# One core, four blocks: decay rows by broadcast DMA, tail decay on the keys, half-size fillers, another step order

## The reference

```python
mixed = jax.nn.silu(_causal_conv(hidden @ w_qkv, conv_w))      # q, k: 16 heads of 128; v: 32 heads of 128
g = -jnp.exp(A_log) * jax.nn.softplus(a + dt_bias)             # one decay per token and value head
def step(state, xs):
    q_t, k_t, v_t, g_t, b_t = xs
    state = state * jnp.exp(g_t)[..., None, None]
    kv = jnp.einsum('bhk,bhkv->bhv', k_t, state)
    delta = (v_t - kv) * b_t[..., None]
    state = state + jnp.einsum('bhk,bhv->bhkv', k_t, delta)
    out = jnp.einsum('bhk,bhkv->bhv', q_t, state)
    return (state, out)
# out * silu(z), RMS norm, times norm_gamma, @ w_out
```

## Time and profile before

| | before |
|---|---|
| median of three executions | 1450.89 us |
| profiled execution | 1452.2 us, its span 1450.4 us |
| TensorE (PE) busy | 1304.9 us, 90% |
| weight loads (PEld) busy, beside PE | 872.4 us, 60% |
| VectorE (DVE) busy | 962.6 us, 66% |
| ScalarE (ACT) busy | 792.2 us, 55% |
| GpSimd (POOL) busy | 750.8 us, 52% |
| mean granted TensorE clock | 0.973 of full speed |
| step 0 up to the first scan product | to 96.6 us |
| steps 1 to 16 | 96.6 to 1036 us |
| the other three blocks | the remaining 414 us |

### The profile page before, as it was taken

How to read it: one execution, slowest core, us unless ns; L and a number is a source line. 1 busy time by engine, 2 the same in 40 slices (tenths; PEclk the granted TensorE clock), 3 DMA queues, 4 the chain that set the end, 5 groups by cost and what they waited for, 6 DMA issues and landing times. The chain is left out here.

```text
span 1450.4 us, 24932 instructions
## 1 busy us (share of the span) xinstructions
PE 1304.9 (90%) x8680; PEld 872.4 (60%) x8680; DVE 962.6 (66%) x1918; ACT 792.2 (55%) x1944; POOL 750.8 (52%) x1245
## 2 busy tenths in 40 slices
PE   6768999999999999999999999988898899899893
PEld 4356666666666666666666666665545466545672
DVE  5847778787787877878778787774602366641454
ACT  3546676666766667666666666665432365420120
POOL 1675776857758667585676856761000000117363
PEclk9969999999999999999999999999999999999997
DMA  2534355354453544535445354364201950202687
GB/s 81 134 64 114 64 152 142 90 150 113 133 138 93 150 117 128 143 88 150 117 129 143 88 150 117 114 145 157 66 0 27 374 160 1 81 13 104 137 185 185
DMA packets 233180, 171.71 MB, mean 118 GB/s; under 512 B 163746, under 2 KB 202998, under 8 KB 230240
## 3 DMA queue, kind: packets, MB, share of 16 engines
q1 hardware_dynamic: 226912, 161.59, 41.3%
q0 software_dynamic: 6144, 8.53, 3.3%
HBM read 104.64 MB, written 65.83 MB: 118 GB/s over the span
## 5 line engine op out<-in xcount | busy, mean ns | idle before, releaser
L1267 DVE SCALAR_TENSOR_TENSOR heads_y<-psum_banks,gdn_conv_w,heads_y 128x1021 f32<-128x1021 f32 (+2 forms) x192 | 244.6, 1275 | 11.3 <-ACT heads_y L1072 6.8
L776 PE MATMUL psum_banks<-main_hT,gdn_w_in 128*128 128x512 f32 x512 | 242.6, 608 | 6.1 <-DMA gdn_w_in<-in_w_in 4.0
L1562 POOL TENSOR_TENSOR heads_XT<-heads_XT,heads_tmp 128x126 f32<-128x126 f32 (+22 forms) x496 | 205.6, 414 | 38.9
L1559 POOL TENSOR_TENSOR heads_tmp<-heads_XT,heads_A 128x126 f32<-128x126 f32 (+22 forms) x496 | 180.7, 364 | 39.8
L776 PEld LDWEIGHTS psum_banks<-main_hT,gdn_w_in 128*128 128x128 f32 x512 | 97.0, 195 | 95.8 <-issue 91.5
L1530 POOL TENSOR_TENSOR heads_og<-heads_og,heads_fac 128x512 f32<-128x512 f32 x60 | 60.5, 1039 | 138.7 <-DVE heads_fac L1333 138.7
L890 PE MATMUL psum_banks<-heads_w_z,main_hT 128*128 128x256 f32 x512 | 122.9, 383 | 0.0
L1095 ACT ACTIVATE heads_O<-psum_banks,heads_coef 128x128 f32<-128x128 f32 x224 | 69.9, 364 | 95.8 <-PE psum_banks L807 95.4
L1072 ACT ACTIVATE heads_y<-psum_banks,gdn_conv_w 128x1024 f32<-128x1024 f32 x64 | 71.4, 1116 | 89.6 <-PE psum_banks L776 89.6
L1288 DVE SCALAR_TENSOR_TENSOR heads_S<-heads_S,heads_coef,psum_banks 128x128 f32<-128x128 f32 x192 | 57.4, 340 | 85.6 <-PE psum_banks L830 85.2
L1278 DVE SCALAR_TENSOR_TENSOR heads_X<-psum_banks,heads_coef,heads_v_s 128x128 f32<-128x128 f32 x224 | 67.9, 345 | 65.3 <-PE psum_banks L805 65.3
(11 more groups left out here) (291 smaller groups left out, 2994.9 us busy)
## 6 DMA issues: line engine op xcount, KB each, us to landing
values_by_tokens<-heads_v_s SPq DMA_DIRECT2D x64, 256.0 KB, 4.1
heads_v_s<-values_by_tokens SPq DMA_DIRECT2D x16, 1024.0 KB, 5.6
outputs_by_features<-heads_ogT SPq DMA_DIRECT2D x120, 128.0 KB, 2.4
heads_ogT<-outputs_by_features SPq DMA_DIRECT2D x30, 512.0 KB, 3.7
main_w_gu<-in_w_gu SPq DMA_DIRECT2D x4, 2816.0 KB, 21.1
gdn_w_in<-in_w_in SPq DMA_DIRECT2D x16, 512.0 KB, 5.3
heads_A<-kk_blocks SPq DMA_DIRECT2D x64, 128.0 KB, 4.8
keys_by_tokens<-heads_k_tok SPq DMA_DIRECT2D x64, 128.0 KB, 3.3
```

The source lines that it names most:

```text
L776: ins = pe.matmul(out[:, half * 512:(half + 1) * 512], w_in[:, kd_, j * P:(j + 1) * P], hT[:, kd_, half * 512:(half + 1) * 512], start=kd_ ...
L1267: dve.scalar_tensor_tensor(y[j][:, shift:T], src[:, 0:T - shift], conv_w[:, head, j, t:t + 1], y[j][:, shift:T], ALU.mult, ALU.add).then_i ...
L1559: pool.tensor_tensor(tmp[:, 0:n, 0:m], bc_last(XT[:, 0:n, j], m), bc_mid(A0[:, j, j + 1:BLK], n), ALU.mult).then_inc(solve_step.sem, 1)
L1562: pool.tensor_tensor(XT[:, 0:n, j + 1:BLK], XT[:, 0:n, j + 1:BLK], tmp[:, 0:n, 0:m], ALU.add).then_inc(solve_step.sem, 1)
```

## The change

Four things are changed, all in the steps:

1. The cumulated sums of head h come by one transfer that copies the row of 2048 numbers to all 128 partitions, straight into `Dm`. The 16 matmuls of `decay0` to `decay3` are gone. VectorE adds the mask in place, from and to SBUF. ScalarE applies exp with a bias for each partition (the negative sum), so in 16 instructions of 128 columns, not 4 of 512. The transfer waits until the inverse of the head before is done with `Dm`, and is first in a step's transfer order.
2. The tail decay is put on the keys: ScalarE makes `k_tail` from the keys of the chunk ahead of its need, Dt is gone, and the state update is two products of 128 columns with two sets of weights, where it was one of 256.
3. Projections, gate products and output products may be split in two (`p0.0`, `p0.1`), to stand in two rows.
4. The order tables of TensorE, ScalarE, VectorE, GpSimd and the transfers are other ones.

```diff
 PE_PLAN = banked(rows("""
-0: z0/0
-1: p0/-1 p1/-1
-3: z1/1
-4: z2/2 norm_q/3
-5: p2/-1
-6: decay0/3 decay1/2 decay2/0 decay3/1
+0: z0/3 p0.0/-1
+1: p0.1/-1 p1.0/-1
+2: p1.1/-1
...
 ACT_PLAN = rows("""
-7: kk0 exp0 kk1 exp1
-10: exp2 exp3 gamma
+9: kk1 exp0
+10: exp1 y6a
+14: diagonal exp2 u6a norms
+15: exp3
...
 DVE_PLAN = rows("""
-5: vt1 decay0 decay1 decay2
-6: decay3
-8: tap10 tap11 tap12 factors turn
+6: decay0 vt1 decay1
+7: factors norm_q tap10
+8: tap11
+9: turn tap12
+10: decay2 decay3
...
-20: inverse0 out0 tap31 out1
-22: out2 tap32 inverse1 out3
+20: attn1 tap31
+21: inverse0 inverse1
+22: tap32 out0 out1 out2 out3
...
+SP_PLAN = """gates inverse_out inverse_in values_out products_out values_in products_in outputs_out0 kt_out outputs_in0 outputs_out1 w_z kt_in outputs_in1 w_in w_o""".split()
+POOL_PLAN = """pow norm0 norm1 q_root norm2 scale norm3 solve""".split()
...
             def gate_rows(h):
-                for sign, rows in enumerate([row_to, row_from]):
-                    src = cum_rows[sign, IT * h:IT * (h + 1)].rearrange("(g s) t -> g s t", g=4)
-                    sp.dma_start(rows[h % 2][sign:P:32], src).then_inc(s_rows[h % 2], 16)
+                src = cum_rows[IT * h:IT * (h + 1)].rearrange("(o s) t -> o (s t)", o=1)
+                sp.dma_start(flat(Dm[:]), src.to_broadcast([P, IT * P])).then_inc(rows_in.sem, 16)
...
                     if c < C - 1:
-                        if c == 0:
-                            pe.wait_ge(kt_loaded.sem, kt_loaded.end(h - 1) * 16)
-                        pe.wait_ge(dt_ready.sem, dt_ready.done(h, f"dt{c}"))
-                        pe.matmul(flat(bank_a[:, 0:2]), k_tok[old][:, c], flat(Dt[:]), start=True, stop=True).then_inc(a_full.sem, 1)
+                        pe.wait_ge(tail_ready.sem, tail_ready.done(h, f"kt{c}"))
+                        for e in range(HD):
+                            ins = pe.matmul(bank_a[:, e], k_tail[c % 2][:, e], Dl[:, e], start=True, stop=True)
+                        ins.then_inc(a_full.sem, 1)
...
+            def tail_keys(h, c):
...
+                for e in range(HD):
+                    i = c * HD + e
+                    ins = act.activation(k_tail[c % 2][:, e], k_tok[(h - 1) % 2][:, c], ACT.Copy, scale=coef[:, TAIL, h - 1, i:i + 1])
+                ins.then_inc(tail_ready.sem, 1)
...
                 if name.startswith("exp"):
-                    b = bank_of(h, f"decay{u}")
-                    act.wait_ge(free[b].sem, free[b].done(h, f"decay{u}"))
-                    part = flat(Dm[:, 4 * u:4 * u + 4])
-                    act.activation(part, part, ACT.Exp).then_inc(dm_ready.sem, 1)
+                    act.wait_ge(dm_masked.sem, dm_masked.done(h, str(u)))
+                    for it in range(4 * u, 4 * u + 4):
+                        ins = act.activation(Dm[:, it], Dm[:, it], ACT.Exp, bias=coef[:, NCUM, h, it:it + 1])
+                    ins.then_inc(dm_ready.sem, 1)
...
+                if name.startswith("decay"):
+                    dve.wait_ge(rows_in.sem, rows_in.end(h) * 16)
+                    part = Dm[:, 4 * u:4 * u + 4]
+                    dve.tensor_tensor(part, part, bc_mid(limit[:], 4), ALU.add).then_inc(dm_masked.sem, 1)
```

More of the change, by code:

```diff
@@ L204 @@
 PE_PLAN = banked(rows("""
-0: z0/0
-1: p0/-1 p1/-1
+0: z0/3 p0.0/-1
+1: p0.1/-1 p1.0/-1
+2: p1.1/-1
 3: z1/1
-4: z2/2 norm_q/3
-5: p2/-1
-6: decay0/3 decay1/2 decay2/0 decay3/1
-7: p3/-1 kk0/3
-8: attn0/1 kk1/3
-9: attn1/2
-10: y6a/3 y6b/0
-12: p4/-1
-13: p5/-1 u6a/3 u6b/0
-14: z3/1
-16: y7_0/0 p6/-1 p7/-1
-18: y7_1/3 u7_0/0
-19: out0/2
-20: u7_1/3
-21: out1/1
-22: out2/2 out3/1
+4: z2.0/2 norm_q/3
+5: z2.1/2 p2.0/-1
+6: p2.1/-1 p3.0/-1
+7: p3.1/-1
+8: kk0/3 attn0/2
+9: kk1/1
+10: z3.0/1 y6a/3 y6b/0 p4.0/-1
+11: p4.1/-1
+12: p5.0/-1
+13: p5.1/-1
+14: u6a/3 u6b/0 z3.1/1
+15: attn1/2 y7_0/3
+16: p6/-1
+17: p7.0/-1
+18: p7.1/-1
+19: y7_1/0 u7_0/1
+20: out0/3 u7_1/1 out1.0/2
+21: out1.1/2
+22: out2/0 out3/1
 """))
@@ L230 @@
 6: kk1/0
-7: decay0/3 decay1/0 decay2/1 decay3/2 p6/-1 p7/-1
+7: p6/-1 p7/-1
 8: attn0/1
@@ L254 @@
 ACT_PLAN = rows("""
-1: q_silu z0 q_square v0_silu base0
-4: v1_silu z1 z2
-6: keys base1
-7: kk0 exp0 kk1 exp1
-10: exp2 exp3 gamma
-11: y6a
-12: y6b
-13: base2 diagonal norms
-14: u6a
-15: u6b
-16: z3 y7_0
+0: z0 q_silu q_square
+1: base0
+3: v0_silu
+4: z1 v1_silu
+5: keys z2
+6: base1
+8: kk0
+9: kk1 exp0
+10: exp1 y6a
+11: gamma
+13: y6b base2
+14: diagonal exp2 u6a norms
+15: exp3
+16: z3 u6b
+17: y7_0
 18: base3
-19: y7_1 u7_0
+19: u7_0 y7_1
 20: u7_1
@@ L291 @@
 DVE_PLAN = rows("""
-0: kt variance
+0: variance kt
 2: tap00
-3: tap01 tap02
-4: vt0 norm_q
-5: vt1 decay0 decay1 decay2
-6: decay3
-8: tap10 tap11 tap12 factors turn
-11: ot0 attn0
-13: scales tap20
-14: tap21 tap22 attn1
-15: ot1
+3: tap01
+4: tap02
+5: vt0
+6: decay0 vt1 decay1
[3 more added lines that the diff above has]
+10: decay2 decay3
+12: attn0 ot0
+13: tap20
+14: scales
+15: tap21 tap22
+16: ot1
 19: tap30
-20: inverse0 out0 tap31 out1
-22: out2 tap32 inverse1 out3
+20: attn1 tap31
+21: inverse0 inverse1
+22: tap32 out0 out1 out2 out3
 """)
@@ L353, in plan, with unit @@
     return {0: PE_FIRST, 1: PE_SECOND, HK + 1: PE_LAST}.get(h, PE_PLAN)
+def unit(name):
+    return name.partition(".")[0]
 def bank_of(h, name):
-    return next(b for row in plan(h) for n, b in row if n == name)
+    return next(b for row in plan(h) for n, b in row if unit(n) == name)
 def bank_plan(h, bank):
-    return [name for row in plan(h) for name, b in row if b == bank and belongs(h, name)]
+    return list(dict.fromkeys(unit(name) for row in plan(h) for name, b in row if b == bank and belongs(h, name)))
 def pe_row(h, k):
@@ L478, in heads @@
     Dl = a.sb("Dl", [P, HD, P])
-    Dt = a.sb("Dt", [P, HD, P])
+    k_tail = [a.sb(f"k_tail{i}", [P, HD, P]) for i in range(2)]
     og = [a.sb(f"og{i}", [P, IT, P]) for i in range(2)]
@@ L772, in _, with project @@
         def _(pe):
-            def project(u, out):
+            def project(u, out, piece=None):
                 j, half = u // 2, u % 2
-                for kd_ in range(KD):
+                for kd_ in range(KD) if piece is None else [piece]:
                     ins = pe.matmul(out[:, half * 512:(half + 1) * 512], w_in[:, kd_, j * P:(j + 1) * P],
                                     hT[:, kd_, half * 512:(half + 1) * 512], start=kd_ == 0, stop=kd_ == KD - 1)
-                if half:
+                if half and piece != 0:
                     ins.then_inc(pair_full.sem, 1)
@@ L852, in product @@
                     pe.wait_ge(act_ready.sem, act_ready.done(h, "sq"))
-                elif name == "decay0":
-                    pe.wait_ge(s_rows[par], 32 * (h // 2 + 1))
-                    for g in range(1, 4):
-                        more = free[bank_of(h, f"decay{g}")]
-                        wait(pe, more, more.ahead(h, f"decay{g}"))
                 elif name.startswith("flip"):
```

120 lines of the change are left out of this document (60 added, 60 removed).

## The result

The changed kernel takes 1443.91 us (median of seven runs, 1434.1 to 1447.7) where the kernel before, run beside it, takes 1451.13: a ratio of 0.9935, 95% interval 0.9912 to 0.9959. It is faster, by 0.65%, where 2.3% were forecast, and it lies outside the range of 1403 to 1440 us. Its executions differ more among themselves than those of before, from 1434.1 us at a mean granted clock of 0.970 to 1447.7, and the profiled one (1447.3 us, clock 0.959) is the second slowest of the seven, so the profile shows less gain than the medians.

The account below looks back on a forecast made before the run. TensorE's order, with waits for the scan's way through ScalarE and VectorE, was taken as the bound. Twelve inner steps (-29.4) and the other steps (-4.4) gave -33.8 us from 1452.2: 1418.4, put at 1417 against the median; range 1403 to 1440.

Parts of the forecast that it names:

- Step 15, "+1.0": Step 15, without projections to fill with: eleven rows empty where eight were, +2.1 us, less the decay's 1.1: +1.0.
- The inner step, "57.9": Inner step, new order walked with old durations: -1.10 - 4.30 + 2.95 (seven new waits) = -2.45, so 57.9 us.
- "I take 1.0" for four exps: ScalarE, inner step: four exps of 128 columns take 1.0 us, between 0.9 (as the squares) and 1.24 (two pairs).
- "Decay products, gain 1.10": Row 6 of the inner step: 32 TensorE passes go, gaining 1.10 us a step.
- "State update 0, Dt gone 0.33": Inner step: the split state update costs 0, and 0.33 us of waits for Dt go.
- "Gaps 4.3 less new waits 2.95": Inner step: 4.3 us of TensorE's old waits can all go; seven new waits on ScalarE or VectorE add 2.95.
- the argument for B: Rival, all steps: only the decay products' time is gained, other waits return; 15 x 1.10 = 16.5, 1434 us, chance 0.25.
- Steps 1 and 2, "-2.0" and "-2.4": Step 1, with the late inverse, gains 2.0 us (0 to 3); step 2, in the inner order, gains 2.4.
- Rival C: Inner steps: the ring of scales, elimination, store, load and turn back to scales becomes the bound; 62 us, 1475 total, chance 0.10.
- Step 16 and the untouched blocks, "-1.0" and "0": Step 16, without decay and with gate halves in two gaps, gains 1.0 us; the other blocks change by 0.
- rival D: State update: 14 more weight loads a step stand bare at 0.13 us each, 1.8 a step; 1446 us, chance 0.02.
- C's sign: VectorE idling at turn for the loaded blocks would show the elimination's ring closed and the forecast wrong.

## Why the prediction was wrong, step by step

The direction was right and the gain forecast nearly five times too large (34 for 7 us of the medians). Three steps of the prediction failed: step 15 had no term for the clock, steps 1 and 2 were taken as inner steps, and the walk of the inner step had one wait at half its size and one not at all. Five terms carry the 28.5 us between the -33.8 forecast and the -5.3 of the profiled executions.

**Step 15, "+1.0" (8.1 us).** I counted its empty rows and no clock. The +1.0 is +2.1 for three more empty rows less the decay's 1.1. The order costs 1.85 (52.91 for 51.06, both at 1.00), so that part was near; the decay's 1.1 brought 0.7 at most (50.12 in the old order everywhere, 51.25 with it in step 15 alone, for 50.86 before, all at 0.97). The fall of the clock is 7.1 on top, shown by the same instructions at 0.86 and at 1.00. That more empty rows bring longer idle stretches stood in the sum; what the granted clock may do behind them did not. Of four executions with the new order in step 15 and nothing added, three fell (0.86, 0.91, 0.91) and one did not; of ten with the old order there and nothing added, seven stand at 0.97, one at 0.93 and two at 1.00. So deep falls went with the thinner step, but not each time. "TensorE: Matmul & The Clock Gate" of the Trainium skill, section "What's actually happening", says that the clock is gated by how busy TensorE has been; I had read that page for its weight loads only. By it a fall is a thing to expect in a step thinned out; three of these four traces agree and one doesn't.

**The inner step, "57.9" (7.3 us).** It measured 58.42. In the prediction's own count (start to start, less the work) the seven waits come to 3.1 us for 2.95, but not each where the walk put it. Row 8 costs 1.08 for 0.5: from 590.77 to 594.50 are 3.73 us for 2.65 of work, of which the bracket shows 0.37. Rows 9 and 10 cost the 0.3 forecast, row 11 0.43 for 0.7, rows 14 and 15 0.1 to 0.2 for 0.3 each, row 12 nothing, row 18 0.96 for 0.85 (its bracket shows 0.79). Beside these stands a wait that no term names: behind the products with S of chunk 5, in row 14, the starts are 0.80 and 0.63 us apart for 0.43 each, 0.57 lost where the kernel before lost 0.11 there. With these 0.1 and 0.5 the 57.9 comes to 58.5, within 0.1 of what was measured. What the second product waits for there is open. The other 0.07 a step are three steps of 58.6 to 58.8.

**"I take 1.0" for four exps.** They take 1.28, 1.1 us a step more than in the sum. What that alone cost is not measured. The wide exps take away row 18's wait and leave those of rows 8, 11 and 14 as they are; a share in proportion (2.6 us more on ScalarE cost 1.1) would be an estimate of 0.5 us. I had gone by the squares, the nearest row, against the 1.24 that the pairs gave. The Trainium skill had it: "ScalarE: Activation LUTs", section "What ACT_TABLE_LOAD costs", gives an activation with a bias per partition some 0.28 us and 0.83 ns a column, with its neighbour overlapping by 0.093. By that one would take 0.39 us and four 0.39 + 3 x 0.29 = 1.27, an estimate from the page's figures; the trace agrees with 389 ns on the profile's page and 1.26 to 1.28 for four. The squares have no such operand, the pairs with a scale per partition do: those were the nearer row.

**The split of that sum was wrong, and that the sum was near is luck.** "Decay products, gain 1.10": alone they make a step 0.56 longer, as the exps double the wait for Dl. "State update 0, Dt gone 0.33": 0.16 lost. "Gaps 4.3 less new waits 2.95", 1.35 net: the order brings 2.5 (60.94 to 58.42), and without the halves all of that and more is gone (61.49). A free place on TensorE is worth nothing in a row where TensorE waits for the others anyway; in the old order 1.10 off it in row 6 only let it reach row 9 sooner, to wait 2.5 us for Dl. One number in the argument for B is a slip: with 2.95 us of new waits for 4.3 of old, the walk counts 5.5 us lost, not 4.2.

**Steps 1 and 2, "-2.0" and "-2.4" (6.5 us).** I took them as inner steps. They took 122.3 us before, and 125.1, 123.2 and 122.8 in the three executions that have the changed kernel's steps 1 and 2, so some 2 of the 6.5 us are scatter; what is shown is that the 4.4 were not gained. They hang on GpSimd's elimination, which in step 1 begins 44 us into the step (140.1 from 95.7) and holds up `factors` of step 2. With it cut short, step 2 falls from 67.1 to 59.6 us; moving the others' work only carried the wait from step 1 to step 2. Rival C named this ring, and bound it to the inner step, where it never decided.

**Step 16 and the untouched blocks, "-1.0" and "0" (2.1 and 4.5 us).** Behind the last mark the work is the same, and the granted clock 0.93 for 0.95. Over the sixteen profiled executions it takes 411 to 419 us whatever stands before; filling step 15 did not change it. This was not a consequence that the runs could tie to the change; what sets the clock there is open. Step 16 takes 43.5 us undisturbed. With both new parts in the old order it takes 42.08 at the same clock, 0.26 less than before, so the new order costs it 1.4; the gain forecast from gate halves in two gaps did not come.

**What held.** Rows 2 and 17 closed and row 11 down from 0.62 to 0.4, the state update in 0.44 (rival D denied), `turn` without a wait in an inner step, the mask never waiting for the broadcast. In step 15 `turn` did wait for the inverse's blocks, 2.19 us before 944.03: C's sign, at a place that the walk did not cover. How much of step 15 it costs was not measured.
